# Fusion attention of a two-branch embedding kernel: scores from row groups of 64, joint K and Q products, biases inside the product

## The reference

```python
h = jnp.concatenate([image(x), text(x_txt)], axis=1)            # 64 x 205 x 64
h = h + attention(_layernorm(h, axis=-1), Wq, bq, Wk, bk, Wv, bv, Wo, bo)
h = h + experts(_layernorm(h, axis=-1), W1, b1, Wg, bg, Wd, bd)

def attention(x, Wq, bq, Wk, bk, Wv, bv, Wo, bo):               # 4 heads of 16
    q, k, v = (heads(x @ W.T + b) for W, b in ((Wq, bq), (Wk, bk), (Wv, bv)))
    attn = jax.nn.softmax(jnp.einsum('bhnd,bhmd->bhnm', q, k) * 16 ** -0.5, axis=-1)
    out = jnp.einsum('bhnm,bhmd->bhnd', attn, v).transpose(0, 2, 1, 3).reshape(B, N, C)
    return out.astype(jnp.bfloat16).astype(jnp.float32) @ Wo.T + bo
```

## Time and profile before

| | us |
|---|---|
| median of 3 timed runs | 2439.25 (2419.43 to 2443.64) |
| the profiled execution: its time | 2400.28 |
| its span, first to last instruction | 2398.5 |
| attention loop, first to last write of `at_QP` (64 samples) | 1520.2 to 1981.2 |
| mean granted TensorE clock | 0.944 of full speed |

### The profile page before, as it was taken

One profiled execution on the slowest core, in us unless ns is written; L12 is line 12 of the kernel. 1 busy time (PEld: TensorE's weight loads), 2 busy tenths in 40 slices (PEclk: granted clock), 3 DMA queues, 4 the chain that ended last, 5 costly groups with the idle time before them and its releaser, 6 DMA issues. The chain is left out here.

```text
span 2398.5 us, 61351 instructions
## 1 busy us (share of the span) xinstructions
PE 2091.4 (87%) x19889; PEld 1736.8 (72%) x19889; DVE 1799.1 (75%) x5716; ACT 1472.5 (61%) x3226; POOL 1198.4 (50%) x1518
## 2 busy tenths in 40 slices
PE   6999999947999999999999981688888885999998
PEld 6999999846888888888888871566666664666665
DVE  4655555345888888888888875688888883888888
ACT  2222222102888888888888874567666665666663
POOL 3433333213777777777777755344444433433441
PEclk8999999975999999999999995699999996999999
DMA  2000003000000000000000000000000000000000
GB/s 89 14 14 14 19 25 68 5 1 1 2 3 2 3 2 3 2 2 2 2 2 2 2 2 0 1 0 0 0 0 0 0 0 1 10 9 11 9 9 11
DMA packets 39663, 20.58 MB, mean 9 GB/s; under 512 B 29508, under 2 KB 38852, under 8 KB 39366
## 3 DMA queue, kind: packets, MB, share of 16 engines
q1 hardware_dynamic: 39466, 18.00, 3.1%
HBM read 14.63 MB, written 3.36 MB: 8 GB/s over the span
## 5 line engine op out<-in xcount | busy, mean ns | idle before, releaser
L439 PE MATMUL im_c<-im_a_hi,im_w 128*128 128x256 f32 (+2 forms) x1920 | 427.9, 317 | 14.5 <-POOL im_a_lo L349 14.5
L439 PEld LDWEIGHTS im_c<-im_a_hi,im_w 128*128 128x128 f32 x1920 | 321.0, 190 | 31.5 <-POOL im_a_lo L349 14.7
L439 PE MATMUL im_c<-im_a_lo,im_w 128*128 128x256 f32 (+2 forms) x960 | 303.0, 316 | 0.0
L1041 POOL TENSOR_TENSOR tx_KB<-tx_KF,tx_head_rows 128x1248 fp32r<-128x1248 f32 x128 | 290.4, 2268 | 23.3 <-PE tx_scores_t L1326 15.2
L343 POOL TENSOR_TENSOR im_rstd<-im_var_eps,im_power 128x4 f32<-128x4 f32 x64 | 68.7, 1073 | 286.7 <-DVE im_var_eps L278 286.7
L902 DVE TENSOR_REDUCE tx_mpad<-tx_scores 77x8 fp32r<-77x616 f32 x256 | 202.1, 790 | 2.6 <-PE tx_maxT L1314 1.9
L272 DVE BATCH_NORM_STATS2 im_stats<-im_h 128x6 f32<-128x128 f32 (+1 forms) x192 | 47.6, 303 | 190.7 <-ACT im_h L384 111.1
L439 PEld LDWEIGHTS im_c<-im_a_lo,im_w 128*128 128x128 f32 x960 | 182.7, 190 | 8.4
L1172 ACT ACTIVATE tx_PT<-tx_scores_t 77x624 f32<-77x624 f32 x256 | 176.2, 688 | 16.8 <-PE tx_scores_t L1326 4.6
L1326 PE MATMUL tx_scores_t<-tx_QP,tx_KB 128*77 128x78 f32 x2048 | 184.0, 240 | 0.0
L1326 PEld LDWEIGHTS tx_scores_t<-tx_QP,tx_KB 128*77 128x77 f32 x2048 | 172.3, 150 | 9.1 <-issue 0.3
(11 more groups left out here) (308 smaller groups left out, 6096.9 us busy)
## 6 DMA issues: line engine op xcount, KB each, us to landing
im_x<-x SPq DMA_DIRECT2D x16, 384.0 KB, 3.4
out<-h_img SPq DMA_DIRECT2D x32, 64.0 KB
tx_toks<-x_txt SPq DMA_DIRECT2D x1, 1925.0 KB
im_raw<-L_tok_conv_w SPq DMA_DIRECT2D x1, 1280.0 KB, 8.7
out<-h_txt SPq DMA_DIRECT2D x32, 38.5 KB
im_raw<-L_tok_conv_w SPq DMA_DIRECT2D x1, 960.0 KB, 4.8
im_raw<-L_tok_conv_w SPq DMA_DIRECT2D x1, 640.0 KB, 5.9
tx_raw_W<-L_txt_W SPq DMA_DIRECT2D x2, 256.0 KB, 6.5
```

What stands on the lines that cost most here:

```text
L439: last = pe.matmul(acc[:, :, d0:d1], w[c][:, slot, part], img[:, b0_:b1_, d0 + shift:d1 + shift, kj:kj + J], start=opens, stop=closes)
L1041: pool.tensor_tensor(KB[:, q % 2, t], KF[:, t].bitcast(F32).unsqueeze(1).broadcast_to([P, HPT, QW]), head_rows[:].unsqueeze(2).broadcast_t ...
```

## The change

`fusion_attention` is rewritten.
- **Row groups.** `KB` and POOL's multiplications for it are gone. A score product takes one head's 64 partitions of Q and K directly (`head`). `score` goes from two products of 412 columns over 128 partitions to four of 206 over 64, `score_t` stays at four of 206, now over 64. The two heads of a tensor write to different banks; `PT` and `scores` are ordered by j, then t. The banks before were ordered by t, then j.
- **Joint K and Q.** Both tensors of K lie in one bank (412 columns), both of Q in another. ACT takes each low part in one instruction instead of two, DVE cuts each in one instead of two. `maxT` moves into the bank of `scores`, and V and y share a bank, which makes set_v and add_y one instruction each.
- **Biases** come from two rows of ones in `xT1`, a second transposed copy (97 rows, written by a second ACT copy), against bias rows in the weights' low part.
- **Normalisation** moves: DVE makes the statistics, POOL adds epsilon, takes the power, subtracts the mean and multiplies; ACT no longer normalises.
- **Order.** Each operation has its own lag, and PE, DVE, ACT and POOL new orders. All 70 steps are written out, with no hardware loop.
- `h_img` and `h_txt` become halves of one buffer `h`; the unused rows 77 to 127 of the text half are zeroed by POOL in the image stage's setup. Fewer, wider loads bring the biases.

Cut to its core (setup of weights and masks, and functions whose body stays alike, left out):

```diff
+                    pool.wait_ge(zeroed, 6)
+                    pool.memset(below_text, 0.0).then_inc(zeroed, 1)
...
+        for r in A_BIAS:
+            for k, m in enumerate(("bq", "bk")):
+                heads = self.b_raw[r:r + 1, k * A_HALF:(k + 1) * A_HALF].rearrange("a (h g) -> a h g", g=A_GROUP)
+                src = wts[m].rearrange("(a h c) -> a h c", a=1, c=A_DH)
+                for copy in range(3):
+                    q.dma_start(heads[:, :, copy * A_DH:(copy + 1) * A_DH], src).then_inc(self.loaded, 16)
+            q.dma_start(self.b_raw[r:r + 1, 2 * A_HALF:], row(wts["bv"])).then_inc(self.loaded, 16)
...
+        xT = sb("xT", [P, 2, SEQP], F32R)
+        xT1 = sb("xT1", [BIAS_ROWS, 2, SEQP], F32R)
+        k_low, q_low = sb("k_low", [P, A_TENSORS, SEQP], F32R), sb("q_low", [P, A_TENSORS, SEQP], F32R)
+        KF = sb("KF", [P, 2, A_TENSORS, SEQP], F32R)
+        PT = sb("PT", [P, 2, A_HPT, WIDE])
+        maxT = scores[:, 0, 0:WIDE].rearrange("p (t s) -> p t s", t=A_TENSORS)
+        x_and_k = p.psum(ctx, "at_x_and_k", [P, 512])
+        of_q = p.psum(ctx, "at_of_q", [P, 512])
+        v_and_y = p.psum(ctx, "at_v_and_y", [P, 2, D])
+        k_rows = x_and_k[:, 0:WIDE].rearrange("p (t s) -> p t s", t=A_TENSORS)
+        q_rows = of_q[:, 0:WIDE].rearrange("p (t s) -> p t s", t=A_TENSORS)
...
+                def join_max(m):
+                    if live(m):
+                        dve.wait_ge(max_turned, m + 1)
+                        if m >= 2:
+                            dve.wait_ge(scored_t, (m - 1) * 2)
+                        dve.tensor_tensor(QP[:, m % 2, :, 0:SEQ], maxT[:, :, 0:SEQ], QF[:, m % 2, :, 0:SEQ].bitcast(F32),
+                                          ALU.add).then_inc(q_set, 1)
+                def cut_k(m):
+                    if live(m):
+                        dve.wait_ge(k_low_set, m + 1)
+                        if m >= 2:
+                            dve.wait_ge(scored_t, (m - 1) * 2)
+                        dve.tensor_tensor(KF[:, m % 2], k_rows, k_low[:].bitcast(F32), ALU.subtract).then_inc(k_cut, 1)
+                def cut_q(m):
+                    if live(m):
+                        dve.wait_ge(q_low_set, m + 1)
+                        dve.tensor_tensor(QF[:, m % 2], q_rows, q_low[:].bitcast(F32), ALU.subtract).then_inc(q_cut, 1)
...
+                        dve.tensor_tensor(both_tiles(m), both_tiles(m), v_and_y[:], ALU.add).then_inc(y_added, 1)
...
+                def step(n):
+                    find_max(n + 1, 0)
+                    add_y(n - 2)
+                    row_stats(n + 4)
+                    find_max(n + 1, 1)
+                    cut_k(n + 2)
+                    join_max(n + 1)
+                    mean_and_var(n + 4)
+                    cut_q(n + 2)
+                    normalise_o(n)
+                    set_v(n + 1)
...
+                def deviation(m):
+                    if live(m):
+                        pool.wait_ge(aggregated, m + 1)
+                        pool.tensor_scalar(var_eps[:], mean_var[:, m % 2, :, 1], EPS, None, ALU.add).then_inc(eps_set, 1)
+                        pool.wait_ge(eps_set, m + 1)
+                        pool.tensor_tensor(rstd[:], var_eps[:], power[:], ALU.pow).then_inc(rstd_set, 1)
+                def norm_rows_of(m):
+                    if live(m):
+                        wide = [P, 2, D]
+                        pool.tensor_tensor(centred[:], both_tiles(m), mean_var[:, m % 2, :, 0].unsqueeze(2).broadcast_to(wide),
+                                           ALU.subtract).then_inc(z_centred, 1)
+                        pool.wait_ge(z_centred, m + 1)
+                        pool.wait_ge(rstd_set, m + 1)
+                        pool.tensor_tensor(z[:], centred[:], rstd[:].unsqueeze(2).broadcast_to(wide), ALU.mult)\
+                            .then_inc(z_set, 1)
...
+                def step(n):
+                    cut_x(n + 3)
+                    deviation(n + 4)
+                    norm_rows_of(n + 4)
...
+                def set_xT(m):
+                    if live(m):
+                        act.wait_ge(x_turned, m + 1)
+                        if m >= 2:
+                            act.wait_ge(v_made, m - 1)
+                        act.activation(xT[:, m % 2, 0:SEQ], x_and_k[:, 0:SEQ], ACT.Copy).then_inc(xT_set, 1)
+                        act.activation(xT1[0:D, m % 2, 0:SEQ], x_and_k[0:D, 0:SEQ], ACT.Copy).then_inc(xT1_set, 1)
+                def low_k(m):
+                    if live(m):
+                        act.wait_ge(k_made, m + 1)
+                        if m >= 1:
+                            act.wait_ge(k_cut, m)
+                        act.activation(k_low[:], k_rows, ACT.Identity, bias=none[:], scale=lo_rows[:, 1:2])\
+                            .then_inc(k_low_set, 1)
...
+                def step(n):
+                    exp(n, 1)
+                    low_k(n + 2)
+                    copy_out(n)
+                    low_q(n + 2)
+                    hi_x(n + 3)
+                    set_oT(n - 1)
+                    exp(n + 1, 0)
+                    set_xT(n + 3)
...
+                def take(bank, read, count):
+                    if bank in held:
+                        pe.wait_ge(*held[bank])
+                    held[bank] = (read, count)
...
+                def project(m, rows, wgt, made):
                     for t in range(A_TENSORS):
+                        cols = slice(t * P, (t + 1) * P)
+                        pe.matmul(rows[:, t], wgt[:, 0, cols], xT[:, m % 2], start=True, stop=False)
+                        last = pe.matmul(rows[:, t], wgt[0:BIAS_ROWS, 1, cols], xT1[:, m % 2], start=False, stop=True)
+                    last.then_inc(made, 1)
...
+                def score(m, tile):
+                    if live(m):
+                        at, n = TILES[tile]
+                        if tile == 0:
+                            pe.wait_ge(k_cut, m + 1)
+                            pe.wait_ge(q_cut, m + 1)
+                            if m >= 1:
+                                pe.wait_ge(q_set, m)
+                        else:
+                            pe.wait_ge(max_set, m * 2 + 1)
+                        for t in range(A_TENSORS):
+                            for j in range(A_HPT):
+                                head = slice(j * A_GROUP, (j + 1) * A_GROUP)
+                                last = pe.matmul(scores[0:n, j, t * SEQP:(t + 1) * SEQP], QF[head, m % 2, t, at:at + n],
+                                                 KF[head, m % 2, t], start=True, stop=True)
+                        last.then_inc(scored, 1)
...
+                                head = slice(j * A_GROUP, (j + 1) * A_GROUP)
+                                last = pe.matmul(scores_t[0:n, j, t * SEQP:(t + 1) * SEQP], KF[head, m % 2, t, at:at + n],
+                                                 QP[head, m % 2, t], start=True, stop=True)
...
+                def step(n):
+                    project_k(n + 2)
+                    project_o(n - 2)
+                    score(n + 1, 1)
+                    weigh(n)
+                    project_q(n + 2)
+                    turn_max(n + 1)
+                    turn_outs(n)
+                    turn_o(n - 1)
+                    score_t(n + 1, 0)
+                    project_v(n + 1)
+                    turn_x(n + 3)
+                    score(n + 2, 0)
+                    score_t(n + 1, 1)
+                for n in range(-4, B + 2):
+                    step(n)
...
+        h = p.sb("h", [P, B, 2, D])
+        h_img, h_txt = h[:, :, 0], h[0:S_TXT, :, 1]
```

More of the change, by code:

```diff
@@ L1503 @@
 EXPERTS = 8
+A_BIAS = (D, D + 32)
 def live(n):
@@ L1898, in _ @@
+                for n in range(-4, B + 2):
+                    step(n)
             @block.tensor
             def _(pe):
-                def score(m, par, tile):
-                    at, n = TILES[tile]
-                    if tile == 0:
-                        pe.wait_ge(k_split, m * 2 + 2)
-                        pe.wait_ge(qk_cut, m * 4 + 4)
-                    if due(m * 2 + tile):
-                        pe.wait_ge(max_set, m * 2 + tile)
-                    for t in range(A_TENSORS):
-                        last = pe.matmul(scores[0:n, t, 0:A_HPT * SEQP], QF[:, par, t, at:at + n],
-                                         KB[:, par, t].rearrange("p j s -> p (j s)"), start=True, stop=True)
-                    last.then_inc(scored, 1)
@@ L2039, in _, with turn_x @@
-                each_step(pe, step)
+                held = {}
+                def take(bank, read, count):
+                    if bank in held:
+                        pe.wait_ge(*held[bank])
+                    held[bank] = (read, count)
+                def turn_x(m):
+                    if live(m):
+                        pe.wait_ge(x_cut, m + 1)
+                        take("x_and_k", xT1_set, m + 1)
+                        for tile, (at, n) in enumerate(TILES):
```

(26 more changed lines are left out.)

506 lines of the change are left out of this document (180 added, 326 removed).

## The result

| | before | after |
|---|---|---|
| median of the timed runs, us | 2429.34 (4 runs) | 2518.02 (4 runs, 2505.44 to 2520.63) |
| ratio to before, 95% interval | 1 | 1.0436 (1.0347 to 1.0525) |
| span of the profiled execution, us | 2398.5 | 2516.0 |
| first to last write of `at_QP`, us | 461.0 | 578.4 |
| mean granted TensorE clock | 0.944 | 0.835 |

A forecast was written before the change was run, and what follows sets the result against it. PE's order and waits were taken to bound the kernel. Saving 61 x (7.23 - 6.37) = 52.5 us, net 49 after one-time costs, gave 2439.25 - 49 = 2390 us, range 2335 to 2440.

The forecast's parts named there:

- What bound the old kernel: Attention loop: PE's order and its waits set the 7.23 us step, some 2.3 us of it waiting.
- The wait on Q's cut: Old attention step: PE's weight loads stand still 0.69 us until DVE has cut Q.
- that for `at_QP`: New attention step: PE's one long wait, for the write of `at_QP`, forecast at 0.3 to 0.7 us.
- The other two: Old PE waits on the first exponential (0.61 us) and ACT's xT copy (0.65 us), forecast to be covered by PE's work.
- The step that failed: Attention loop: the new step was priced at the full clock, giving 6.37 us.
- if the products over half the array let the granted clock fall: Rival, attention loop: a step costs about 10.0 us, the kernel 2610 us with all 61 steps; chance 0.06.
- A change of partition count: PE in the attention loop: each change costs about 0.18 us, seven per step where the old order had two.
- No gain from overlap: Score products: 128-wide loads set the pace, so four still cost 0.44 us, or 0.35 with 77 weight columns.
- the overlap rival: Rival, score groups: row groups run at once and halve, PE waits for ACT, step 5.92 us, 2363 us; chance 0.24.
- 6.37: Attention loop: forecast new step in us, from one `score_t` start to the next; steps of 6.1 to 6.7, chance 0.46.
- The walk: Attention loop: sum of PE's products, changes and waits in order from one `score_t` start to the next, 6.37 us.
- Setup, lead and straight code: Outside the steady loop: 3 us once for lead and longer normalisation, 0.5 for setup, nothing for fetching straight code.

The follow-up runs named there:

- e1_full_rows: Changed kernel with every score product over all 128 partitions instead of one head's 64, both heads summed: 2321.02 us, ratio 0.9599.
- e3_bursts: Changed kernel with 32 extra 512-column products over 128 partitions ahead of `project_q` for samples 8 and 40: 2476.91 us.
- e10_65_rows: Changed kernel with every score product over partitions 0 to 64, both heads of a tensor on the same rows: 2564.64 us.
- e2_before_groups: Kernel before with `score` and `score_t` over one head's 64 partitions, still from POOL's `KB`, banks ordered by head: 2560.18 us, ratio 1.0589.
- e5_changes_only: e1_full_rows with one tiny product over 64 partitions and 8 columns ahead of each of the four score groups of a step: 2424.91 us.
- e6: Changed kernel with both heads' score products on the same partitions 0 to 63, so no overlap of row groups: 2616.99 us.
- e7: Changed kernel with `score` still over 64-partition row groups but `score_t` over all 128 partitions: 2551.89 us.
- e8: Changed kernel with the four products of `project_q` made twice, the first result overwritten: 2574.40 us, ratio 1.0615.
- e4_full_kb: Changed kernel with POOL's zero-padded `KB` back and `score` and `score_t` reading it over 128 partitions: 2331.39 us, ratio 0.9628.

## Why the prediction was wrong

- **What bound the old kernel** was right: e1_full_rows, the new order without the row groups, takes 6.00 us per step where the old took 7.23. The wait on Q's cut went, and that for `at_QP` came, 0.52 us of the 0.3 to 0.7 forecast. The other two shrank and were not gone: that on xT is 0.23 in the timeline of e3_bursts, that on the exponential costs 0.2 in e1_full_rows.
- **The step that failed** is the one that took the clock of before for that of after. It had been put as a rival, "if the products over half the array let the granted clock fall", with a chance of 0.06, and set aside because the clock was 1.00 with PE busy for 83% and PE's share would rise. PE's share did rise, to 99%, and it said nothing: e1_full_rows and e10_65_rows both have PE busy for over 94% and differ in the clock. What the runs showed in its place is that the clock of the stage hangs on the rows of the score products: 1.00 over 128, 0.50 over 64 or 65. The word was wrong as well: the clock did not fall in the loop of after. Both kernels enter it at 0.50; that of before rose at about 1540 (0.80 is the mean of its first 100 us), that of after did not.
- **The price of that rival** was 10.0 us per step and 2610 us. Measured: 9.24 and 2518.02. 10.0 is the step of the old order at 1.2 GHz. In the new order it is 9.91 without overlap (e10_65_rows) and 9.24 with it, so most of the difference is the overlap that the forecast left out. In the old order the groups gained nothing: e2_before_groups still has 10.0.
- **A change of partition count** was priced at 0.18 us, and e5_changes_only gives at most that: 0.36 for two of them with the tiny product.
- **No gain from overlap** was wrong: four products take 0.31 us in place of 0.44, and the step at the full clock is 5.71, under the 5.92 of the overlap rival and far under 6.37. Most of the 0.21 to that rival is ACT's copies of xT: `project_k` starts 1615.51 - 1613.64 = 1.87 us after `score_t`, where the rival has 2.05. The reason given, that 128-wide loads set the pace, does not hold between row groups.
- **The walk** itself was sound. Without the four further changes PE would be ahead of ACT, and `project_k` waits as in the overlap rival, until 2.05; the prediction's own terms from there on, without the change before the second `score`, give 2.05 + 0.44 + 0.38 + 0.35 + 0.18 + 0.83 + 0.44 + 1.245 = 5.92 (1.245 is the way from `turn_max` over `join_max` to the next `score_t`). e1_full_rows took 6.00, with `project_k` at 1701.96 - 1699.86 = 2.10. A plain 6.37 - 4 x 0.18 = 5.65 would miss that wait.
- **A slip in counting**: the prediction has 46 products in a step before and 50 after. The windows views have 744 in 100 us at 7.23 per step and 631 at 9.24, which is 54 and 58. Nothing in its sum hangs on them.
- **Setup, lead and straight code** at 3.5 us: the growth of the loop is 117.4 of the span's 117.5, so nothing measurable outside the loop.

The terms that were mis-sized would not have turned the forecast gain into a loss; the two forms with full rows did gain, 3.7 and 4.0%. The clock alone turned it: it costs (9.24 - 5.71) us x 61 steps = 215 us, against the 93 that the change would gain at the full clock, (7.23 - 5.71) x 61.

What stays open is where between 65 and 128 partitions, and between eight score products of a step and none, the boundary lies; why the first burst of e3_bursts was held for 13 steps and the second for one; and why the clock rises for moments in e2, e3, e5 and e6 and never in the steady steps of after, e7, e8 and e10.

## What to carry to other kernels

Before a product is cut to fewer partitions, look at the granted clock of its stage and at how it got there: this loop comes out of an idle stretch at 1.2 GHz, and without extra products put in, the clock rose and stayed only with its score products over all 128 rows, zeros included. PE's busy share was no guide to that, since it was highest where the clock was low (99% at 0.50, 94% at 1.00). So forecast such a change at both clocks, and keep the full-row form (here with POOL making the padded copy beside the path) as the version to beat.

## What the runs showed of the hardware

- The same instructions with score products over 65 rather than 128 partitions left the granted clock at 0.50 for the whole stage (9.91 against 6.00 us per step; one execution of e10_65_rows, four of e1_full_rows).
- With rows padded with zeros the clock was 1.00 (e4_full_kb).
- Two row groups of 64 overlapped, with loads of 128 columns: 0.31 us for four products against 0.44. The Trainium skill, TensorE: Matmul & The Clock Gate, Part 3, recommends such groups for small contractions, as their products run at once. The traces agree on the overlap.
- A change of the partition count cost at most 0.18 us at the full clock (e5_changes_only), and eight more of them per step did not keep the clock from rising.
- A burst of 32 full products raised the clock while it ran, from 0.50 to 1.00 within its 8.33 us. The loop with row groups then held it for 13 steps and lost it.
